# Turning normed tokens by VectorE from rows loaded back in 512-byte pieces, in an attention and mixture-of-experts layer

## The reference

```
xn  = layernorm(x)
q, k, v = silu(xn @ Wq), silu(xn @ Wk), silu(xn @ Wv)     # 16 heads of 32
o   = chunked linear attention of q, k, v, decay per head, chunks of 128 tokens
gate = (xn @ Wg1) @ Wg2
o   = rmsnorm per head of (o * sigmoid(gate)), times norm_w
y   = o @ Wo
top 2 of 8 experts by softmax(xn @ Wg), at most CAP slots per expert
ffn = sum over the two of gate value * (relu(xn @ w1[e]) @ w2[e])
out = x + y + ffn
```

## Time and profile before

| | |
|---|---|
| median of 3 runs | 2051.66 us (2050.84 to 2051.95) |
| the profiled execution's own time | 2050.61 us |
| its span in the profile | 2048.7 us |
| TensorE busy | 2013.3 us, 98% |
| VectorE, ScalarE, GpSimd busy | 906.7, 552.7, 731.3 us |
| TensorE's share of the chain that ended last | 96% |
| granted TensorE clock, mean | 0.995 |

### The profile page before, as it was taken

The page is one execution under the profiler, slowest core; times in us unless marked ns, Lnnn a source line. Parts: engine busy times, 40 slices in busy tenths (PEclk is TensorE's granted clock), DMA queues, the critical chain, the costliest instruction groups (busy, mean ns, idle before and its releaser), DMA issues.

```text
span 2048.7 us, 27795 instructions
## 1 busy us (share of the span) xinstructions
PE 2013.3 (98%) x11096; PEld 1659.5 (81%) x11096; DVE 906.7 (44%) x1791; ACT 552.7 (27%) x985; POOL 731.3 (36%) x600
## 2 busy tenths in 40 slices
PE   7999999999999999999999999999999999999996
PEld 6788888888888888888888888888888888888885
DVE  7776777776752224324323422422342234324311
ACT  5322222223332123123212312421242123123210
POOL 4454535553632214233242431332142224324211
PEclk9999999999999999999999999999999999999998
DMA  7012021202352125224233421531162125224021
GB/s 233 31 63 84 24 82 63 84 17 89 94 161 48 34 47 159 36 64 109 70 68 65 133 45 53 127 67 30 47 158 39 40 49 154 40 60 116 21 30 20
DMA packets 85500, 151.36 MB, mean 74 GB/s; under 512 B 18304, under 2 KB 18304, under 8 KB 85360
## 3 DMA queue, kind: packets, MB, share of 16 engines
q1 hardware_dynamic: 61312, 105.64, 16.0%
q0 software_dynamic: 24048, 43.76, 12.6%
HBM read 109.82 MB, written 39.53 MB: 73 GB/s over the span
## 4 chain that ended last, share of the span: by engine, by line
PE 96%; DVE 2%; issue 1%; POOL 1%; ACT 0%; DMA 0%; SPq 0%; ACTq 0%; POOLq 0%
PE bank L1199 50%; PE bank L1463 34%; PE bank L1322 4%; PE bank L1498 2%; PE bank L1248 2%; PE bank L1206 1%; PE bank L1289 1%; PE bank L1311 1%; PE bank L1305 1%; DVE oT_lo L981 0%; DVE xnT_lo L864 0%; PE bank L1282 0%; ACT oT_hi L716 0%; POOL out_rows L612 0%; PE bank L1333 0%
## 5 line engine op out<-in xcount | busy, mean ns | idle before, releaser
L1146 DVE SCALAR_TENSOR_TENSOR h_lo<-bank,h_hi 128x512 fp32r<-128x512 f32 x256 | 176.7, 690 | 758.8 <-ACT h_hi L804 716.3
L599 POOL DMA_INDIRECT gathered<-xn_rows,gather_row x304 | 321.7, 1058 | 475.0 <-DVE x_blocks L1022 294.1
L1199 PE MATMUL bank<-xT_hi,w_hi 128*128 128x512 f32 x1024 | 398.7, 389 | 0.3 <-issue 0.2
L1199 PE MATMUL bank<-xT_hi,w_lo 128*128 128x512 f32 x1024 | 398.4, 389 | 0.0
L1199 PE MATMUL bank<-xT_lo,w_hi 128*128 128x512 f32 x1024 | 398.4, 389 | 0.0
L1463 PE MATMUL bank<-w_hi,h_hi 128*128 128x512 f32 x1024 | 398.3, 389 | 0.0
L1463 PE MATMUL bank<-w_lo,h_hi 128*128 128x512 f32 x1024 | 398.3, 389 | 0.0
L1463 PE MATMUL bank<-w_hi,h_lo 128*128 128x512 f32 x1024 | 398.3, 389 | 0.0
L804 ACT ACTIVATE h_hi<-bank 128x512 fp32r<-128x512 f32 x256 | 153.0, 597 | 813.3 <-PE bank L1199 729.6
L612 POOL DMA_INDIRECT out_rows<-y,add_row x80 | 128.6, 1608 | 550.4 <-ACT y L797 477.5
L1199 PEld LDWEIGHTS bank<-xT_hi,w_hi 128*128 128x128 f32 x1024 | 192.2, 188 | 41.4 <-issue 1.7
(11 more groups left out here) (195 smaller groups left out, 2354.1 us busy)
## 6 DMA issues: line engine op xcount, KB each, us to landing
raw_weights<-in_L_ffn_w SPq DMA_DIRECT2D x256, 256.0 KB
x_in<-in_L_attn_x SPq DMA_DIRECT2D x32, 256.0 KB
xn_rows<-xn SPq DMA_DIRECT2D x32, 256.0 KB, 2.7
x_res<-in_L_attn_x SPq DMA_DIRECT2D x32, 256.0 KB
out_rows<-y_attn SPq DMA_DIRECT2D x28, 256.0 KB, 2.0
gathered<-xn_rows,gather_row POOLq DMA_INDIRECT x304
out_rows<-y,add_row POOLq DMA_INDIRECT x80, 5.9
attn_raw<-in_L_attn_Wq SPq DMA_DIRECT2D x4, 256.0 KB, 5.0
```

The costliest lines, as they stand in the source:

```text
L599: pool.indirect_dma_start(xg[:, nth % 2, q * P:(q + 1) * P], None, xn_pieces, bass.IndirectOffsetOnAxis(ap=gather_row[:, col, q:q + 1], ax ...
L1146: v_.scalar_tensor_tensor(h_lo[f % 2][:, 0:n * P], h_bank[f % 2][:, 0:n * P], 0.0, h_hi[f % 2][:, 0:n * P].bitcast(F32), ALU.max, ALU.subt ...
L1199: last = mm(dest, at(left[l], t), at_r(right[r], t), start=(i == 0), stop=(i == n - 1))
```

## The change

1. For tiles 4 to 31, TensorE's transposes are gone. SyncE, once the store of a normed tile has landed, loads it back from `xn_rows` into `x_in` (`reload_xn`): four DMAs per tile, each for 32 tokens. A partition gets 128 features of one token, 512 bytes. VectorE turns the tile in 32x32 blocks into `xn` (`turn_blocks`). A 32x32 block transpose leaves quarters of partitions where the rows put them, and so the features of k-tile t are those with numbers 128q + 32t + d for q in 0 to 3, d in 0 to 31.
2. ACT and VectorE read the turned tile from SBUF (`turned_tile`) instead of PSUM.
3. Tiles 0 to 3 are still turned by TensorE, into the same order, by 16 matmuls of 32 output rows per tile instead of 4 of 128 (`turn_quads`).
4. The rows of Wq, Wk, Wv and of the gate and router weights are loaded in that order; the gate and router weights by 8 DMAs instead of 2.
5. `x_in` is used by the reload as well, so x loads wait for `blocks_turned` and are issued elsewhere. In i=1 SyncE's and VectorE's lists are interleaved anew. In i=2 the casts to `xnT_hi` stand ahead of `oT_high`. In i=3 the states stand ahead of the mean square, and `oT_low(u - 3)`, which i=2 leaves out, comes behind them.
6. The scores' wait for `xnT_lo` and the waits of TensorE around `turn_xn` are gone.

```
+            def reload_xn(t):
+                j = t % TPG
+                sp.wait_ge(xn_stored[j], 16 * (t // TPG + 1))
+                for m in range(QUADS):
+                    rows = xn_dram[t * P + m * 32:t * P + (m + 1) * 32, :].rearrange("r (q d) -> q r d", q=QUADS)
+                    sp.dma_start(x_in[:, j, m * P:(m + 1) * P], rows).then_inc(xn_reloaded[j], 16)
...
             def load_x(t):
-                if t >= TPG:
-                    wait(sp, ("xn_ready", t - TPG + 1))
+                if t >= 2 * TPG:
+                    sp.wait_ge(S["blocks_turned"], t - 2 * TPG + 1)
+                elif t >= TPG:
+                    sp.wait_ge(S["xn_ready"], t - TPG + 1)
...
-            sp.dma_start(small_raw[:, :, 0:HD], wg1.rearrange("(t p) n -> p t n", p=P)).then_inc(S["small_loaded"], 16)
-            sp.dma_start(small_raw[:, :, HD:], w_route.rearrange("(t p) n -> p t n", p=P)).then_inc(S["small_loaded"], 16)
+            for t in range(DT):
+                for cols, source in ((slice(0, HD), wg1), (slice(HD, HD + EXPERTS), w_route)):
+                    sp.dma_start(small_raw[:, t, cols], source.rearrange("(q t d) n -> t q d n", q=QUADS, t=DT)[t]
+                                 ).then_inc(S["small_loaded"], 16)
...
             def xnT_high(t):
                 j = t % TPG
-                act.wait_ge(S["xn_turned"], t + 1)
-                wait(act, ("k_projected", GROUPS * (t // TPG)))
+                if t < TPG:
+                    act.wait_ge(S["xn_turned"], t + 1)
+                else:
+                    act.wait_ge(S["blocks_turned"], t - TPG + 1)
+                    act.wait_ge(S["k_projected"], GROUPS * (t // TPG))
+                a.copy(token_cols(xnT_hi, j), turned_tile(t)).then_inc(S["xnT_hi_made"], 1)
...
+            def turn_blocks(t):
+                j = t % TPG
+                dve.wait_ge(xn_reloaded[j], 16 * QUADS * (t // TPG))
+                v_.transpose(xn[:, j, :], x_in[:, j, :]).then_inc(S["blocks_turned"], 1)
...
-                if i == 2 and g < SUPERS - 1:
-                    pe.wait_ge(S["masked"], HPG * (u + 1))
-                    turn_xn(g + 1, lambda j: pe.wait_ge(S["q_ready" if j == 2 else "k_ready"], u + 2) if j > 1 else None)
                 attend(u)
```

More of the change, by code:

```diff
@@ L241, in build @@
         xn_stored = [sem(f"xn_stored{i}") for i in range(TPG)]
+        xn_reloaded = [sem(f"xn_reloaded{i}") for i in range(TPG)]
         y_stored = [sem(f"y_stored{i}") for i in range(2)]
@@ L406, in _ @@
                     sp.dma_start(slot_rec[:, spare_cols, :], spare_slots[0]).then_inc(S["rec_loaded"], 16)
[L407 to L410, removed]
+                if i == 1:
+                    if g > 0:
+                        store_y(TPG * (g - 1))
+                    if g > 0 and g < SUPERS - 1:
                         store_xn(TPG * (g + 1) + 2)
@@ L1074, in _ @@
                         normalise(t)
+                if i == GROUPS - 1 and g < SUPERS - 1:
+                    states(u)
+                    oT_low(u - 3)
                 if u > 0:
@@ L1085, in _ @@
                         xnT_low(TPG * (g + 1) + j)
+                elif u > 1:
+                    oT_low(u - 2)
                 gate_output(u)
@@ L1230, in weights_arrive, with turn_quads, turn_first_group @@
                 return lambda i: wait(pe, ("attn_w_lo", first + i // 3 + 1)) if i % 3 == 0 and i < 3 * DT else None
-            def turn_xn(g, bank_free=lambda j: None):
+            def turn_quads(dest, source):
+                for t in range(DT):
+                    for q in range(QUADS):
+                        first = q * P + t * HD
+                        last = mm(dest[q * HD:(q + 1) * HD, t * P:(t + 1) * P], source[:, first:first + HD], ident[:, :],
+                                  start=True, stop=True)
+                return last
+            def turn_first_group():
                 for j in range(TPG):
-                    pe.wait_ge(S["xn_ready"], TPG * g + j + 1)
-                    bank_free(j)
-                    turn(xn_bank[j], xn[:, j, :], DT).then_inc(S["xn_turned"], 1)
+                    pe.wait_ge(S["xn_ready"], j + 1)
+                    turn_quads(sc[j], xn[:, j, :]).then_inc(S["xn_turned"], 1)
             def score(u):
@@ L1329, in turn_first @@
                 pe.wait_ge(first_gathered[i], 16)
-                for t in range(DT):
-                    for q in range(QUADS):
-                        rows, first = slice(q * HD, (q + 1) * HD), q * P + t * HD
-                        last = mm(first_bank[i][rows, t * P:(t + 1) * P], y[:, i, first:first + HD], ident[:, :], start=True, stop=True)
-                last.then_inc(S["x_turned"], 1)
+                turn_quads(first_bank[i], y[:, i, :]).then_inc(S["x_turned"], 1)
             pe.wait_ge(S["consts_made"], 6)
-            turn_xn(0)
+            turn_first_group()
             pe.wait_ge(S["xnT_lo_made"], TPG)
```

100 lines of the change are left out of this document (61 added, 39 removed).

## The result

The changed kernel takes 2127.5 us (2125.41 to 2128.97, 4 runs), where the kernel before, on the same chip, takes 2051.3 (2050.84 to 2051.95, 4 runs): a ratio of 1.037, 95% interval 1.035 to 1.039, 76 us slower. The profiled execution has a span of 2125.1 us, and a mean granted clock of 0.979 where it had 0.995. The prediction was 2044.3 with a range of 2040 to 2053.

The account below looks back on a forecast made before the run. TensorE, which hardly ever waits, was taken to bound the kernel. Gains of 1.6 + 2.43 + 3.42 = 7.4 us took the profiled 2050.6 to 2043.2; the runs' median lies 1.05 higher, hence 2044.3, range 2040 to 2053.

Parts of the forecast that it names:

- Step 6: At the start: six more weight issues hidden, first group's quarter transposes 0, row order of Wq, Wk, Wv 0.
- Step 3: Reload chain in i=1: eight issues at 0.48 us, landing 2.1 us; group 1's masks at 130.2 instead of 128.18.
- step 4: Attend waits for later states, 1.3 of 1.75 us given back in group 1; three odd groups gain 2.43, three even 3.42.
- Rival B: Reload landing in i=1: DMA engines can't move 512-byte pieces at issue pace; 12.9 us in six groups, 2057; chance 0.15.
- the gather stretch: Stretch with one tile gathered in 512-byte pieces beside weight loads: 1.35 us a tile, under its issues' 1.9; cited against B.
- Steps 2 and 4: The `xnT_lo` chains on VectorE, behind ACT's casts and behind the states: four subtractions at an estimated 0.65 us each.
- steps 1 and 2: TensorE's transposes and scores' wait gone: ceiling 14.7 us; i=3's gate projection, waiting for the fourth `xnT_lo`, caps it at 11.2.
- rival C: Short reload issues and landings leave only the ACT cast chain ahead of i=3's gate projection: 11.2 off, 2040.5; chance 0.2.

Follow-up runs that it names:

- all loads by quadrants: The changed kernel with reload, Wq, Wk, Wv, gate and router loads rewritten with 32 outermost instead of 4: 2069.3 us, ratio 1.009.
- the reload mended: The changed kernel with only the reload DMAs rewritten as [32][4][128] instead of [4][32][128], slow weight loads kept: 2090.15 us, one run.
- the two runs with GpSimd beside it and without: All loads by quadrants plus paired reloads and y stores first: 2068.13 us; that with VectorE making `kdT` and GpSimd's `qdT` waiting for `xnT_lo`: 2060.15 us.
- the best one: The changed kernel with quadrant loads, paired reloads, `kdT` by VectorE, turns of tiles 2 and 3 behind the states, and Wq, Wk, Wv start reworked: 2041.68 us, ratio 0.9955.
- n = 4: The kernel before with only the rows of Wq, Wk, Wv loaded in 4 runs of 32 rows per DMA: 2074.96 us.

## Why the prediction was wrong

*Step 6, the start, failed first.* It said that the row order "leaves 2 KB rows as they are: 0"; the start cost 31.3 us. I looked at the size of a piece and not at the shape of the DMA. The outermost dimension went from 128 to 4, and the busy share of the DMA engines from 1.06 to 0.26. Undone alone this is worth 29.4 us (70.43 to 41.05); done alone on the kernel before, 24.6. SyncE shared the cost: its issues stretched (11.22 us for Wk's four instead of 1.85), and Wv went out 19 us later.

*Step 3, the reload, failed by the same cause: its term "I take 2.1" for issue to landing, and 0.48 for each issue, were both too small.* Its links can be set beside the changed kernel's group 1, on VectorE and SyncE:

```profile
148.37 0.71 DVE L1007 STREAM_TRANSPOSE turned_odd<-gated 128x512 f32<-128x512 f32 x1
...
153.33 0.96 DVE L893 TENSOR_SCALAR xn<-x_in,moments,rstd 128x512 f32<-128x512 f32 x2
```
```profile
157.44 5.36 SPq L360 DMA_DIRECT2D x_in<-xn_rows  x8
```

From the end of the gate output's transpose (149.08) the reloads start after 8.4 us (step 3: 7.1), eight issues take 5.36 (3.8), and the masks, at 168.01, come after 18.9 (13.2). Of the 5.7 us that are missing, 2.8 had come about by the end of the last issue, and 2.9 are between it and the masks. Attend's wait is 5.67, where step 4 had 1.3. Issue to landing is 2.9 us with 32 outermost, in the kernel with all loads by quadrants; I had 2.1. Rival B named the right place and the right direction, with the wrong cause: it priced the packets (5.5 us for two tiles) on 16 engines. On four engines the pieces of one tile, 1.35 us by the gather stretch, would be 5.4, and two tiles 10.8 (an estimate; from the first reload issue to the masks group 1 takes 10.6). The argument against B, the gather stretch, was of DMAs of another shape, and took for granted that the reloads spread over as many engines.

*Steps 2 and 4: the size of `xnT_lo`.* They took 0.65 a tile from other operations. Alone it is 0.68, which is right; beside GpSimd it is up to 1.77, and four of them take 3.53 in group 1 of the changed kernel and 4.62 with the reload mended. Its price is some 7.1 us, the difference of the two runs with GpSimd beside it and without. With one operand in PSUM this subtraction took 674 to 692 ns in all 32 cases of the kernel before, so its rows could not show the price of two operands in SBUF. The Trainium skill, "SBUF — State Buffer", Who interferes with whom, has VectorE and GpSimd share an SBUF port pair, and an operation of VectorE with two SBUF inputs contend with a GpSimd operation that reads SBUF; these rows agree.

*What no step had: the clock.* The same 4141 instructions of TensorE are busy for 509.5 us in the changed kernel and 492.8 in the best one: 16.7 us, with a mean clock of 0.96 against 1.00. Taken microsecond by microsecond, the busy time times the part of the clock that was not granted is 14.4 us, all of it behind the six long waits (an estimate); for the other 2.3 no cause was looked for. With it the groups can be added up: transposes gone 503.4 - 492.8 = -10.6; the same work longer +16.7; idle 42.5 - 3.6 = +38.9; in all +45.0, measured +44.8.

*What held.* The ceiling and cap of steps 1 and 2: with all late things mended the groups gain 10.5 us (506.9 to 496.4), where 11.2 was the cap by the chain of `xnT_lo`, and the remaining wait is at the place named, 0.5 a group. Step 4's wait of 1.0 to 1.5 us ahead of attend: with the DMAs mended four of the six are 1.0 to 1.3, the other two 2.35 and 2.42. The best version's 2041.7 is near rival C's 2040.5, but that is no proof of C: it took the turns behind the states, `kdT` made by VectorE and another start. The 64 quarter transposes of the first group put its first `xnT_lo` 0.5 us later (11.03 to 11.54), where I had up to 0.4, and its fourth 1.0 (14.11 to 15.10).

*What stays open.* With DMAs mended and nothing else (all by quadrants), the groups are 10.7 us slower than before. Attend's 9.6, the gate's 9.0 and `y_attn`'s 1.5 less the 10.6 of transposes and the 2.5 of the scores' wait give 7.0; PE's busy time is 4.0 above the best version's in the same stretch (496.8 against 492.8), which makes 11.0. Of these 4.0, 1.7 are clock (by the same estimate as above): behind attend's wait of 2.35 us in group 3, at 283.5, it is 0.72 over 6 us, and 1.00 everywhere else. The other 2.3 stay open; they are as large as the 2.3 that the clock does not cover in the changed kernel. The 6.7 us of the changed kernel's start loss that n = 4 alone does not show (31.3 - 24.6) were not split either.

## What to carry to other kernels

Before a rearranged DMA is priced by its bytes and pieces, read its outermost dimension on both sides: with 4 and with 8 some of the DMA engines stood idle, and nesting the same pieces the other way round brought 58 of 76 us back, though not the full rate. Don't put a consumer of fresh DMA data directly ahead of work that the critical engine waits for; two transposes of 0.7 us moved behind the masks and states in VectorE's list were worth 12.4 us. And when an operand moves from PSUM to SBUF, look at who else works in SBUF at that moment. Last, price a wait of several microseconds on TensorE together with the clock that falls in it.

## What the runs showed of the hardware

- Busy share of the DMA engines against the outermost dimension, 10 to 15 us: 0.26, 0.59, 1.10, 1.12 for 4, 8, 16, 128; 98, 195, 239, 309 GB/s. First masks at 63.75, 48.30, 39.84, 39.15.
- DMAs into 32 partitions at a time moved 266 GB/s where 128-partition ones moved 398, in 5 to 10 us, at the same busy share; 128-partition ones with rows in 16 runs of 8 moved 293.
- A 128x512 subtraction on VectorE with both inputs in SBUF takes 0.68 us alone and up to 1.77 beside GpSimd's elementwise products; with one input in PSUM 0.67 to 0.69 always.
- Behind TensorE's six waits of 5.4 to 6.0 us in the changed kernel the granted clock was 0.51 to 0.66 over 6 us. In the groups, behind waits of 0.6 to 1.55 us, it stayed at 1.00. In between it went both ways: in the runs with the reload mended it fell to 0.52 to 0.72 behind waits of 1.94, 2.12, 2.29, 2.32, 2.33, 2.35, 2.38 and 3.10 us, and stayed at 1.00 behind others of 1.90, 1.91, 2.42 and 2.64.
